# Stage of counts in a graph network: upper products on 32-partition strips, and the load of x moved and split

## The reference, cut to what matters

```python
h = jnp.maximum(_layernorm(x, axis=-1), 0.0)          # 100000 x 16
# layer L0, first convolution, for a node whose only edge is its own loop:
h1 = selu(h @ W1 + b1)                                # 16 -> 96
# the second convolution's inputs of that node:
h2 = h1 @ W2                                          # 96 -> 32, and two scores
# and the scores (h @ W1 reshaped * a_src1).sum(-1) of every node, 3 heads
```

## Time and profile before

| | us |
|---|---|
| median of 3 runs | 7763.85 |
| lowest, highest | 7750.85, 7764.83 |
| span of the profiled execution, first to last instruction | 6645.3 |
| mean granted clock of PE over the span, share of full | 0.654 |

### The profile page before, as it was taken

One profiled execution on the slowest core, in us unless ns is written; L12 is line 12 of the kernel. 1 busy time (PEld: TensorE's weight loads), 2 busy tenths in 40 slices (PEclk: granted clock), 3 DMA queues, 4 the chain that ended last, 5 costly groups with the idle time before them and its releaser, 6 DMA issues. The chain is left out here.

```text
span 6645.3 us, 44822 instructions
## 1 busy us (share of the span) xinstructions
PE 2965.9 (45%) x13056; PEld 2260.1 (34%) x13056; DVE 3659.5 (55%) x8917; ACT 1167.0 (18%) x1912; POOL 4320.0 (65%) x3949
## 2 busy tenths in 40 slices
PE   5798699974444344447655443111111002544000
PEld 2477555543333233346644333111111001433000
DVE  8855499976555566654347667433322068876000
ACT  0265454532222233211111100000000000000000
POOL 4666555557762776376657665888888823766776
PEclk9899899985666555556667665555555555776555
DMA  2122222221110322123222212222222234211001
GB/s 41 22 62 70 56 67 67 66 66 12 20 17 14 89 60 65 47 64 100 84 87 60 64 53 72 52 36 36 44 27 27 5 96 154 57 50 37 7 7 44
DMA packets 283354, 350.11 MB, mean 53 GB/s; under 512 B 133518, under 2 KB 204432, under 8 KB 281970
## 3 DMA queue, kind: packets, MB, share of 16 engines
q1 hardware_dynamic: 112158, 295.24, 13.2%
q0 software_dynamic: 169376, 41.40, 7.8%
q10 hardware_dynamic: 1576, 10.60, 0.7%
HBM read 231.06 MB, written 122.29 MB: 53 GB/s over the span
## 5 line engine op out<-in xcount | busy, mean ns | idle before, releaser
L2352 POOL DMA_INDIRECT acc<-l_rows,l_uniq x392 | 624.1, 1592 | 121.0 <-issue 108.6
L2573 POOL DMA_INDIRECT l_ring<-t_last,idx x392 | 392.4, 1001 | 366.5 <-ACTq L2568 207.6
L521 POOL DMA_INDIRECT pay<-in_x,gidx x392 | 460.1, 1174 | 235.4 <-DMA pay<-in_x,gidx 114.3
L2393 PE MATMUL ps_l<-l_msg,l_alike 128*128 128x16 f32 x784 | 176.3, 376 | 962.4 <-DVE l_msg L2456 962.4
L1487 POOL DMA_INDIRECT g_ring<-t_gat,idx x392 | 416.1, 1062 | 278.7 <-issue 110.1
L1817 POOL DMA_INDIRECT r_ring<-t_rel,idx x392 | 414.6, 1058 | 254.6 <-issue 110.3
L809 POOL DMA_INDIRECT t_sort<-pay,c_pos x392 | 384.8, 982 | 296.3 <-DVE c_pos L875 196.3
L901 PE MATMUL ps_c<-plane,c_hit 128*128 128x400 f32 x1568 | 542.6, 499 | 1.2 <-ACT c_hit L827 1.2
L2128 POOL DMA_INDIRECT r_ring<-t_rel,idx x392 | 392.7, 1002 | 224.4 <-issue 110.4
L2338 POOL DMA_INDIRECT l_ring<-t_mix,idx x392 | 426.3, 1087 | 154.6 <-issue 119.1
L2393 PEld LDWEIGHTS ps_l<-l_msg,l_alike 128*128 128x128 f32 x784 | 171.0, 331 | 967.7 <-DVE l_msg L2456 967.7
(11 more groups left out here) (529 smaller groups left out, 8145.0 us busy)
## 6 DMA issues: line engine op xcount, KB each, us to landing
c_rows_d<-row_dst SPq DMA_DIRECT2D x98, 256.0 KB, 3.3
l_keys<-row_at SPq DMA_DIRECT2D x49, 512.0 KB, 4.2
l_typs<-row_typ SPq DMA_DIRECT2D x49, 512.0 KB, 3.7
g_hs<-t_gat SPq DMA_DIRECT2D x30, 660.0 KB, 4.7
acc<-r_zero SPq DMA_DIRECT2D x60, 320.0 KB
t_rel<-r_row SPq DMA_DIRECT2D x30, 640.0 KB, 3.5
r_hs<-t_rel SPq DMA_DIRECT2D x30, 640.0 KB, 4.7
d_gain<-acc SPq DMA_DIRECT2D x30, 640.0 KB, 6.0
```

The lines of the kernel that those rows point to most:

```text
L521: pool.indirect_dma_start(pay[:, s, 8:PAY], None, x, bass.IndirectOffsetOnAxis(gidx[:, s:s + 1], 0)).then_inc(gat_in[s // BATCH], 16)
L2352: pool.indirect_dma_start(acc[r], bass.IndirectOffsetOnAxis(uniq[:, s:s + 1], 0), rows[:, (s // ES) % RR, s % ES, :], None, compute_op=ALU.add
L2573: pool.indirect_dma_start(ring[:, s, :], None, t_last, bass.IndirectOffsetOnAxis(idx2[:, s:s + 1], 0)).then_inc(gat_in[s // BATCH], 16)
```

## The change

The two products of an upper u contract over the 32 partitions (strip u) on which `w1_dense[:, 2u+j]` is not zero, in place of all 128. They are issued in pairs: for j = 0 the strips 2*half and 2*half+1, then for j = 1 the same two. The order of PE becomes down u = 0, down u = 1, the four upper products of u = 0 and 1 of the next step, and the same for u = 2 and 3. The number of products, their columns and the increments of semaphores stay as they were. On SP, the load of x for two chunks on is issued in the first step of a chunk (ahead of that step's store of `row2`, behind the last step's) in place of the last step, and as two DMAs, of partitions 0 to 111 and 112 to 124; `x_in` counts 32 for a chunk.

```diff
-                            dve.wait_ge(x_in[b], 16 * (k // 2 + 1))
+                            dve.wait_ge(x_in[b], 32 * (k // 2 + 1))
...
-                    def up(n, u):
-                        if u == 0:
+                    def up_pair(n, half):
+
+                        if half == 0:
                             hold(pe, copy_ok, n + 1)
-                        to = ps[0:HID, UP + 512 * u:UP + 512 * (u + 1)]
                         for j in range(2):
-                            last = mm(to[:, 256 * j:256 * (j + 1)], w1_dense[:, 2 * u + j], norm_t[:, n % 3],
-                                      start=True, stop=True)
-                        last.then_inc(up_ok, 1)
+                            for u in (2 * half, 2 * half + 1):
+                                strip = slice(32 * u, 32 * (u + 1))
+                                at = UP + 512 * u + 256 * j
+                                last = mm(ps[0:HID, at:at + 256], w1_dense[strip, 2 * u + j], norm_t[strip, n % 3],
+                                          start=True, stop=True)
+                                if j:
+                                    last.then_inc(up_ok, 1)
...
-                        for u in range(4):
-                            if n and u % 2 == 0:
-                                hold(pe, row2_ok, 2 * (n - 1) + u // 2 + 1)
-                            hold(pe, act_ok, 4 * n + u + 1)
-                            for m in range(4):
-                                at = 512 * (u // 2) + (CH + 2) * (4 * (u % 2) + m)
-                                last = mm(ps[:, at:at + WIDE], act_t[:, u, P * m:P * (m + 1)], w2_ext[:],
-                                          start=True, stop=True, skip_group_check=True)
-                            if u % 2:
-                                last.then_inc(down_ok, 1)
+                        for half in range(2):
+                            if n:
+                                hold(pe, row2_ok, 2 * (n - 1) + half + 1)
+                            for u in (2 * half, 2 * half + 1):
+                                hold(pe, act_ok, 4 * n + u + 1)
+                                for m in range(4):
+                                    at = 512 * half + (CH + 2) * (4 * (u % 2) + m)
+                                    last = mm(ps[:, at:at + WIDE], act_t[:, u, P * m:P * (m + 1)], w2_ext[:],
+                                              start=True, stop=True, skip_group_check=True)
+                            last.then_inc(down_ok, 1)
                             if n + 1 < NSUB:
-                                up(n + 1, u)
+                                up_pair(n + 1, half)
...
                         if k >= 2:
                             hold(sp, var_ok, k - 1)
-                        sp.dma_start(xin[0:NPART, k % 2], x.rearrange("(p c) f -> p c f", c=C)[:, k * Q:(k + 1) * Q, :]
-                                     ).then_inc(x_in[k % 2], 16)
+                        rows_in = x.rearrange("(p c) f -> p c f", c=C)[:, k * Q:(k + 1) * Q, :]
+                        for p0, p1 in ((0, 112), (112, NPART)):
+                            sp.dma_start(xin[p0:p1, k % 2], rows_in[p0:p1]).then_inc(x_in[k % 2], 16)
...
                         k = n // PER
+                        if n % PER == 0 and k + 2 < ND:
+                            load(k + 2)
                         if n % PER == PER - 1:
...
-                            if k + 2 < ND:
-                                load(k + 2)
```

More of the change, by code:

```diff
@@ L663, in score @@
                         last.then_inc(score_ok, 1)
-                    def up(n, u):
-                        if u == 0:
+                    def up_pair(n, half):
+                        if half == 0:
                             hold(pe, copy_ok, n + 1)
-                        to = ps[0:HID, UP + 512 * u:UP + 512 * (u + 1)]
                         for j in range(2):
-                            last = mm(to[:, 256 * j:256 * (j + 1)], w1_dense[:, 2 * u + j], norm_t[:, n % 3],
-                                      start=True, stop=True)
-                        last.then_inc(up_ok, 1)
+                            for u in (2 * half, 2 * half + 1):
[5 more added lines that the diff above has]
+                                    last.then_inc(up_ok, 1)
                     flip(0)
                     flip(1)
-                    for u in range(4):
-                        up(0, u)
+                    for half in range(2):
+                        up_pair(0, half)
                     score(0)
```

## The result

The changed kernel is slower: median 7830.3 us of 20 runs (7779.11 to 7916.86) against 7768.77 us of 20 runs of the kernel before (7729.17 to 7832.3), ratio 1.0086, 95% interval [1.0063, 1.0109]. The loss is 49 to 85 us where a gain of 16 was forecast. The range ended at 7766.

The account below looks back on a forecast made before the run. POOL's gathers were taken to bound the kernel, PE's chain being hidden. Waits behind the x loads, 20.2 us, would shrink to 4, a gain of 16: 7763.85 - 16 = 7748, range 7732 to 7766; strips added nothing.

Parts of the forecast that it names:

- POOL is the bound before: End of the phase: POOL's gathers last to about 761, PE's chain ends at 723, so the phase lasts as long as POOL.
- The load of x: POOL's batch waits: loading x earlier and in two pieces cuts 20.2 us of waits to 4, a gain of 16.
- 16 engines in place of 5: DMA of x: 112 partitions get 16 engines where 125 got 5, so the load takes 1.7 us.
- Upper products on strips: PE's steps: between 1.3 us saved and 1.3 us added a step, 0.7 saved taken; over 50 steps 35 us shorter.
- the cold clock behind a wait: PE after the x stall: some 2 us of cold clock a chunk, given back with the stall's 7 us.
- Either way the phase's sum below stays as it is: Phase's sum: unchanged whether strips save or drains add up to 1.3 us a step, as PE's chain is hidden behind POOL.
- The slack I had worked out: PE's steps: they end later than POOL only if one takes over 9.4 us, 1.3 over PE's present 8.1.
- PE becomes the bound: Rival, PE between down and upper products: strips halve its clock, last gather 263 us later, 8027 in all; chance 0.07.
- The rule on drains: PE's array: changing the tiling mode drains the engine, so the upper bound of +1.3 us a step holds for the changes.
- What would show it: Profile signs, among them last gather near 744; wrong if last store follows last gather, clock under 0.8, or POOL awaits `act_t`.
- The last store "near 620 to 665": End of PE's chain: the last store was expected at 620 to 665 in place of 723.
- half of PE's work stays at height 96 and dense: PE's steps: argument against the rival of a half clock, which had a chance of 0.07.

Follow-up runs that it names:

- e2: Kernel before with only the new load of x (first step of a chunk, two DMAs), upper products at full height, old order; ratio 0.9968.
- e1: The kernel before, unchanged, run for a second profile; ratio 0.9995.
- e11: Kernel before with the load of x only split in two (112 and 13 partitions), still issued in a chunk's last step; ratio 0.9993.
- e4: Changed kernel with the upper products contracted over all 128 partitions; new order of PE and new load stay; ratio 0.9957.
- e5: Kernel before with the new load of x and each upper product on its strip of 32, neighbours sharing a strip, old order; ratio 1.0428.
- e7: e2 with POOL waiting, before a batch of gathers, for the landing of the batch before the last, not the last; ratio 0.9965.

## Why the prediction was wrong

- *POOL is the bound before*: right. e2 shortened PE's chain from 741.7 (e1) to 688.1, 54 us, and the stage by 8.
- *The load of x*: right in kind, and in size within the noise. Forecast: gain of 16. Measured: stage 8 to 17 us earlier, ratios 0.9968 and 0.9973, of which 16 us would be 0.9979. Where I put the gain was half wrong: I gave it to 16 engines in place of 5, while e11 suggests, by the stage's end alone, that the place, away from the 800 KB store, is needed. The batches' waits from the 14th batch on add up to 90 us in e1, 102 in e11, 82 in e2. The DMA share was near 1 as forecast: in e2 it is 1.16, 0.81 and 0.83 in the three windows of 1 us from 323 on, and the load with its neighbour store is over.
- *Upper products on strips, bounds of -1.3 to +1.3 us a step*: here the prediction failed. The bounds held at full clock: a step of 6.65 us lies 1.0 below the 7.65 that full height needs when nothing waits (four u of 1.75 and 0.65 for score and flip; 487.57 - 479.93 = 7.64 in e4), drains included, near the 0.7 I took. But the bounds left the clock out of the term, and put it among the rivals at 0.07. At half clock a step takes 12.5, and the steps took (814.3 - 274)/50 = 10.8 us on average. The prediction had priced the cold clock behind a wait at 2 us a chunk. With strips, pauses of 1.1 to 2.6 us brought 10 to 181 us at half clock.
- *"Either way the phase's sum below stays as it is"*: wrong for that reason. The slack I had worked out (9.4 us a step) was right, and was crossed by 1.4 us a step: the next phase came 53 us later than in the second profile of the unchanged kernel, 45 later than in the first. Of the 61 us between these two profiles the stage holds 53, and 61 lies within the 49 to 85 of the ratio. Behind the stage little moved (from there to the end 6987 us in the changed kernel, 6980 in e1).
- *The rival "PE becomes the bound"* had mechanism, place and deciding point right. Its price, 263 us, supposed half clock throughout; two strips at a time had it in part. e5 is what I had priced: half clock throughout, +333 us (0.0428 of 7777), 70 above my figure. That figure charged nothing for the changes of height, 0.45 us a u by the rows above, 90 in 50 steps. Nor did the rival say what starts the half clock: pauses of PE of 1 to 3 us.
- *The rule on drains*, from the Trainium skill (TensorEngine Tiling, Key Properties): the trace agrees. PEld's idle 0.70 and 0.23 us at the changes in e5 show it. The changes cost far less than the clock did.
- *What would show it* named the right signs: the last store after the last gather, the clock under 0.8, POOL waiting for `act_t`. All three came true. The last store "near 620 to 665" did not, even where the clock was kept: 688.1 in e2, 703.7 in e4.
- My argument against, "half of PE's work stays at height 96 and dense", is refuted by the windows at 20.00 of 20.00 busy and clock 0.50. Here, dense in time was not enough to bring the clock back.

## What to carry to other kernels

Before an edit lowers how much of PE's array a product uses, price the whole stage at half clock, and see whether the slack in front of the true bound holds it; a narrower product that runs sooner can still make every other product of the stage slower. Look for pauses of the engine as short as 1 or 2 us: at full height each cost 7 us at half clock or less (e4), on strips up to 181. Strips for half of the products kept 0.94 here; height 64 did in the profiled run, but four of its ten runs were 1.3% or more above that one. Neither gave PE's chain anything over full height in the old order (last store 705.0 and 722.6, for 688.1). And read the end of a phase before its windows: a chain that ends 37 us early is worth nothing shortened, but is the one to ruin.

## What the runs showed of the hardware

- When 16 of a step's 54 product records contracted over 32 rows, PE's granted clock fell to 0.50 (1.2 GHz) behind pauses of 1.1 to 2.6 us, as it does at full height, but then stayed there with PE busy all the time, 120.00 of 120.00 us from 680 to 800. At full height (e4) it was back within 7 us each time. The mean over 270 to 700 us was 0.50 to 0.68 on strips, 0.94 with 64 rows, 0.98 at full height.
- Strips of 32 rows ran side by side: at full clock 1.11 us for eight records on two strips, 1.12 for sixteen on four, 1.96 for eight on one half.
- With more gathers in flight on POOL (two batches in place of one, e7), the last gather came 10 us earlier and the last store 74 us later than in e2 (762.2 for 688.1), with PE idle for no wait up to 1.2 us. That is one profile of each, and the times don't differ (0.9965 and 0.9968).
